# Two row-maxima jobs put into one slot of an attention schedule

## What is computed

```python
logits = jnp.einsum('nhid,nhjd->nhij', q, k) * scale
logits = logits + causal            # 1e9 * (tril - 1)
attn = jax.nn.softmax(logits, axis=-1)
out = jnp.einsum('nhij,nhjd->nhid', attn, v)
x = layernorm(x + out @ Wo + bo)
```

## Time and profile before

| | us |
|---|---|
| median of 3 runs (963.89 to 965.67) | 964.39 |
| profiled execution, its own time | 962.76 |
| its span, first to last instruction | 960.9 |
| granted TensorE clock, mean of the span | 0.923 |

### The profile page before, as it was taken

How to read it: one execution, slowest core, us unless ns; L and a number is a source line. 1 busy time by engine, 2 the same in 40 slices (tenths; PEclk the granted TensorE clock), 3 DMA queues, 4 the chain that set the end, 5 groups by cost and what they waited for, 6 DMA issues and landing times. The chain is left out here.

```text
span 960.9 us, 25894 instructions
## 1 busy us (share of the span) xinstructions
PE 800.2 (83%) x10965; PEld 530.8 (55%) x10965; DVE 590.0 (61%) x1026; ACT 689.4 (72%) x953; POOL 624.5 (65%) x393
## 2 busy tenths in 40 slices
PE   5789999999999999999999999999986666542490
PEld 3345555666566666656666665666655554332390
DVE  5686777656666665666566665656776477375015
ACT  4357777888888878888888888788994766341263
POOL 6256768889888887888888888877004664113350
PEclk9799999999999999999999999999998997555695
DMA  6211133220230122023011301310006200040252
GB/s 169 46 35 35 29 78 74 57 45 2 51 84 2 35 44 59 2 51 83 4 36 24 78 2 42 72 23 2 2 2 211 68 1 2 0 89 24 77 183 89
DMA packets 58060, 48.31 MB, mean 50 GB/s; under 512 B 6602, under 2 KB 54344, under 8 KB 57814
## 3 DMA queue, kind: packets, MB, share of 16 engines
q1 hardware_dynamic: 56198, 43.60, 19.1%
q0 software_dynamic: 1024, 1.45, 0.5%
q10 hardware_dynamic: 720, 1.57, 0.5%
HBM read 16.64 MB, written 5.26 MB: 23 GB/s over the span
## 5 line engine op out<-in xcount | busy, mean ns | idle before, releaser
L670 POOL TENSOR_TENSOR prob_lo<-prob,prob_hi 128x896 f16<-128x896 f32 (+2 forms) x286 | 518.4, 1833 | 127.7 <-ACT prob L501 109.8
L559 DVE TENSOR_REDUCE part_max<-psum 128x2 f32<-128x1024 f32 (+1 forms) x320 | 334.2, 1060 | 110.9 <-PE psum L359 78.6
L498 ACT ACTIVATE prob_hi<-psum 128x1024 f16<-128x1024 f32 (+1 forms) x320 | 297.3, 930 | 119.2 <-PE psum L407 114.7
L501 ACT ACTIVATE prob<-psum 128x1024 f32<-128x1024 f32 (+1 forms) x320 | 296.9, 930 | 0.0
L404 PE MATMUL psum<-high 128*128 128x512 f16 (+3 forms) x640 | 224.5, 351 | 23.8 <-DVE part_max L559 8.3
L430 PE MATMUL psum<-v,prob_hi 128*128 128x65 f16 x2176 | 232.3, 193 | 3.9 <-DVE prob_lo L598 3.0
L434 PE MATMUL psum<-v,prob_lo 128*128 128x65 f16 x2176 | 230.4, 194 | 0.0
L432 PE MATMUL psum<-v,prob_hi 128*128 128x64 f16 x2176 | 230.4, 192 | 0.0
L430 PEld LDWEIGHTS psum<-v,prob_hi 128*128 128x128 f16 x2176 | 198.9, 98 | 45.3 <-issue 15.7
L407 PE MATMUL psum<-mixed 65*128 65x512 f16 (+3 forms) x640 | 220.6, 349 | 0.0
L432 PEld LDWEIGHTS psum<-v,prob_hi 128*128 128x128 f16 x2176 | 200.3, 97 | 13.3
(11 more groups left out here) (226 smaller groups left out, 1084.6 us busy)
## 6 DMA issues: line engine op xcount, KB each, us to landing
high<-kq SPq DMA_DIRECT2D x128, 128.0 KB
mixed<-kq SPq DMA_DIRECT2D x64, 128.0 KB
ew<-in_L_ffn_W SPq DMA_DIRECT2D x32, 256.0 KB
expert_rows<-heads_out SPq DMA_DIRECT2D x1, 1032.0 KB, 8.3
e_xe<-expert_rows SPq DMA_DIRECT2D x4, 258.0 KB, 3.7
prob<-in_L_attn_x SPq DMA_DIRECT2D x4, 256.0 KB, 6.7
mixed<-shift SPq DMA_DIRECT2D x64, 1.0 KB
eb<-in_L_ffn_b SPq DMA_DIRECT2D x1, 1024.0 KB
```

The source lines that it names most:

```text
L498: act.activation(m.prob_hi[i % HI_RING][:, 0:u.width], src, ACT.Exp, scale=EXP_SCALE)
L501: act.activation(m.prob[i % PROB_RING][:, 0:u.width], src, ACT.Exp, scale=EXP_SCALE)\
L559: last = dve.tensor_reduce(m.part_max[:, g % 2, :, r, c:c + 1], src[:, :, col:col + width], AX, ALU.max)
L670: pool.tensor_tensor(m.prob_lo[i % LOW_RING][:, c], m.prob[i % PROB_RING][:, c], m.prob_hi[i % HI_RING][:, c], ALU.subtract).then_inc(low_ ...
```

## The change

In the stretches of the pairs 1 to 7, where two max jobs of the same group follow each other in the list of jobs, the first of the two moves into the slot of the second. The two are then run back to back. No job is added or removed, and the jobs keep their order.

```diff
+def beside(at, jobs):
+    at, k = list(at), 0
+    while k + 1 < len(jobs):
+        if jobs[k].kind == jobs[k + 1].kind == "max" and jobs[k].group == jobs[k + 1].group:
+            at[k] = at[k + 1]
+            k += 1
+        k += 1
+    return at
+
+
 def spread_jobs(plan, jobs, begin, end):
 
     at = [begin + k * (end - begin) // len(jobs) for k in range(len(jobs))]
+    if begin >= FIRST[1]:
+        at = beside(at, jobs)
     for h, job in zip(at, jobs):
         plan[h].append(job)
     return at
```

## The result

The changed kernel takes 992.85 us (median of 4 runs, 992.41 to 994.53) beside 965.03 us for the kernel before in the same comparison: a ratio of 1.0289, 95% interval 1.0267 to 1.0311. It is slower by 28 us, where 30 had been forecast. Its profiled execution took 992.41 us, its span is 990.4, 29.5 longer than before.

A forecast was written before the change was run, and what follows sets the result against it. TensorE bounds the kernel, busy 82.37 of each 85.25 us period. Savings and new waits sum to +4.3 a period; six periods make 26, pair 1 another 4.3, together +30: 995 us, range 966 to 1020.

The forecast's parts named there:

- Edges: TensorE changing into and out of max jobs: one edge out and one in saved per couple, 16 x 0.20 = 3.2 us per period.
- Old waits: Five places per period where TensorE already waits for a buffer ahead of scores: all 3.4 us taken as removed, 2.9 at least.
- Couples ahead of scores: Even second slots, nine per period in pairs 2 to 7: the next scores wait for a buffer, together 6.45 us.
- The walk: One period followed couple by couple with durations from the old trace, giving each wait of scores or second job.
- Couples behind scores: Odd second slots, seven per period: second job or next scores wait for a buffer, 4.0 us in all.
- the single job behind them: One single max job behind the last couple of group 2: costs another 0.46 us per period.
- Sum: One period of pairs 2 to 7: -3.2 - 3.4 + 6.45 + 4.0 + 0.46 = +4.3 us on 85.25.
- pair 1: First pair's stretch, 36 max jobs in 29 units in place of 40: taken at 4.3 us as well.
- upper bound: Longer waits, old waits worth only 2.9: 14.8 - 6.1 = +8.7 us a period, seven times 61, 1025 us.
- The edges alone: Rival: scores find a buffer, 112 x 0.20 = 22.4 us saved, 942; wins if waits behind couples average below 0.2; chance 0.09.
- The clock: Rival: idle spells drop TensorE to 1.2 GHz in half of 64 cycles, 93 us on top, some 1088; chance 0.04.

The follow-up runs named there:

- kernel with narrow couples: Against the kernel before: couples only in slots ahead of scores where ScalarE reads a 384-wide unit, other max jobs keeping their even spread; 972.70 us, ratio 1.0083.

## Why the prediction was right, step by step

*Edges.* Sixteen couples a period should save 32 edges of 0.10: the count falls from 78 to 46 in the trace. The rule on draining in the Trainium skill, "TensorEngine Tiling (Array Packing)", section "Key Properties", holds here, 0.10 a change, and is outweighed.

*Old waits.* Taken as removed, all 3.4. In the changed kernel three of the five scores wait no more (0.41, 1.13 and 0.72 before). The other two still do, 1.18 for 0.70 and 0.41 for 0.46, but now behind couples, and the forecast counts them there.

*Couples ahead of scores.* The walk gave 0.57, 1.04, 0, 0.27 and 1.18, 1.04, 0.83, 0.61, 0.91, in all 6.45; the trace has 0.60, 1.07, 0, 0.30 and 1.18, 1.07, 0.85, 0.62, 0.95, in all 6.64. None is off by more than 0.04.

*Couples behind scores.* The walk gave 4.0 and 0.46 for the single job behind them; the trace has 0.16, 0.54, 0.77, 0.92, 0.53, 0.44 and 0.55, together 3.9, and 0.43. Three waits of 0.08 to 0.14 beside them are not in this list.

*Sum.* +4.3 a period was forecast, +4.62 came. The mis-sized term is pair 1, taken at another 4.3: its stretch, from the scores of unit 16 to those of unit 44, takes 73.6 us for 71.3, 2.3 more. By the count above its edges fall from 78 to 48, and its waits rise from 6.7 to 12.1, by 5.4, where a later period has some 8 more: TensorE lost more to buffers there before, and the couples replaced more of it. Which waits made way, no run here takes apart. Up to that stretch all kernels that change only the order run the same TensorE instructions, and yet their traces reach it at 76.25 (changed), 78.63 (before) and 76.45 to 78.68 us (the others); so the 2.4 there are no effect of the change. What the change touches thus cost 6 x 4.62 + 2.3 = 30.0, and that this is the +30 of the forecast is in part luck: the periods came out 2 us above their term, pair 1 came out 2 us below. In the upper bound there is a slip that nothing rests on: its waits add up to 15.1, not 14.8.

*Rivals.* The edges alone lose, since the scores behind the nine couples wait 0.74 on the mean, where 0.2 was the mark. The clock stayed at 1.00 in every period; the failure mode that the Trainium skill describes in "TensorE: Matmul & The Clock Gate", section "A second HAM failure mode: psum-queue depth-cycling", did not appear with idle spells of up to 1.2 us. That buffers are the cause is shown from two sides: shortening VectorE's hold took 84% of the loss in a period (4.62 to 0.73) and shortening ScalarE's turned it into a gain (85.41 to 84.78), with the same couples in the same slots. No run changed the number of buffers, or the choice among them alone.

## What to carry to other kernels

Before two jobs that need the same kind of buffer are put side by side to save a switch, count the buffers at that moment: what the couple holds, what the slowest reader still holds, and what the next instruction in TensorE's order wants. The wait is the earliest release less the moment TensorE is ready, and three rows of the old trace give it to a few hundredths of a microsecond. If the switch is worth saving, first shorten the hold, and only in the places that need it: one read fewer from the buffer made the same couples a gain.

## What the runs showed that had not been expected

Splitting ScalarE's two independent Exp passes into a pass and a dependent copy cost 0.26 us a unit of 1024 (2.08 for 1.82), though neither instruction is printed as much longer (1.02 and 1.06): the start of the second moves from 0.92 to 1.12 behind the first. In these rows two passes that depend on each other lose the overlap that independent ones have; the wait between them, the Copy in place of Exp and its other source are not taken apart.

And ScalarE's order of units matters as much as their width: a 384-wide unit is free 1.5 us after its scores (400.71 to 402.22 in the kernel with narrow couples), because the 896-wide unit ahead of it has to be read first.
